# Turned value products with reciprocals through memory in the first attention, and the second attention's first score rounds among its last output products

## What is computed

```python
# first attention: H = 16 heads of D = 64, phi(x) = elu(x) + 1, written as a scan over positions
Q = _phi((x @ Wq + bq).reshape(bs, n, H, D)).transpose(1, 0, 2, 3)
K = _phi((x @ Wk + bk).reshape(bs, n, H, D)).transpose(1, 0, 2, 3)
V = (x @ Wv + bv).reshape(bs, n, H, D).transpose(1, 0, 2, 3)
...
    num = jnp.einsum('bhd,bhde->bhe', qi, KV)
    den = jnp.einsum('bhd,bhd->bh', qi, Ks)
    return ((KV, Ks), num / (den[..., None] + EPS))
...
return out @ Wo + bo
# second attention: 16 heads of 16, keys and values are the context itself
energy = jnp.einsum('nqhd,nkhd->nhqk', q, k)
energy = jnp.where(mask == 0, jnp.float32(-1e+20), energy)
attn = jax.nn.softmax(energy / jnp.sqrt(jnp.float32(EMB)), axis=-1)
out = jnp.einsum('nhqk,nkhd->nqhd', attn, v).reshape(N, Q, EMB)
return out @ W_out.T
```

## Time and profile before

| | |
|---|---|
| median of three runs | 1427.04 us |
| profiled execution | 1428.32 us |
| its span | 1426.3 us |
| TensorE busy | 1361.6 us (95%) |
| VectorE busy | 732.8 us (51%) |
| ScalarE busy | 515.3 us (36%) |
| GpSimd busy | 286.3 us (20%) |
| first attention, first to last projection pair | 13.5 to 331 us |
| second attention, batches in steady state | 14.6 us each |

### The profile page before, as it was taken

One profiled execution on the slowest core, in us unless ns is written; L12 is line 12 of the kernel. 1 busy time (PEld: TensorE's weight loads), 2 busy tenths in 40 slices (PEclk: granted clock), 3 DMA queues, 4 the chain that ended last, 5 costly groups with the idle time before them and its releaser, 6 DMA issues.

```text
span 1426.3 us, 30313 instructions
## 1 busy us (share of the span) xinstructions
PE 1361.6 (95%) x12024; PEld 955.1 (67%) x12024; DVE 732.8 (51%) x1762; ACT 515.3 (36%) x1004; POOL 286.3 (20%) x380
## 2 busy tenths in 40 slices
PE   6999999998999999889998999999999899999996
PEld 5888888885566666556664466575757677777764
DVE  5665555554566665367753122011112555678886
ACT  2212111221455555446654422122121444444444
POOL 2000000101111112388844000000000200124421
PEclk9999999998899999999999999999999999999999
DMA  6300000001222220012200100000000000000001
GB/s 205 62 13 0 1 1 1 1 1 35 46 48 63 53 59 24 2 43 74 62 17 10 56 0 0 0 1 0 0 0 0 3 3 4 13 17 16 16 6 53
DMA packets 35984, 36.04 MB, mean 25 GB/s; under 512 B 11696, under 2 KB 32544, under 8 KB 35856
## 3 DMA queue, kind: packets, MB, share of 16 engines
q1 hardware_dynamic: 35856, 34.23, 9.3%
HBM read 31.61 MB, written 1.86 MB: 23 GB/s over the span
## 4 chain that ended last, share of the span: by engine, by line
PE 67%; ACT 3%; DVE 2%; issue 2%; POOL 2%; DMA 0%; SPq 0%; DVEq 0%; ACTq 0%; POOLq 0%
PE banks L270 32%; PE banks L704 7%; PE banks L688 4%; PE banks L869 3%; PE banks L811 3%; PE banks L824 3%; PE banks L864 3%; PE banks L805 2%; PE banks L720 2%; PE banks L263 2%; ACT area L1248 2%; PE banks L852 2%; ACT area L1325 1%; POOL area L1109 1%; PE banks L762 1%
## 5 line engine op out<-in xcount | busy, mean ns | idle before, releaser
L1582 DVE TENSOR_REDUCE Y_room<-banks 112x2 f32<-112x750 f32 x128 | 115.5, 936 | 91.4 <-PE banks L688 91.4
L1658 DVE TENSOR_REDUCE area<-banks 112x8 f32<-112x896 f32 x96 | 100.2, 1086 | 76.6 <-PE banks L811 76.6
L1248 ACT ACTIVATE area<-banks,Y_room 125x896 f32<-125x896 f32 x96 | 96.7, 1007 | 95.3 <-PE banks L704 95.3
L1325 ACT ACTIVATE area<-banks 112x896 f32<-112x896 f32 x96 | 82.8, 914 | 121.1 <-PE banks L869 121.1
L270 PE MATMUL banks<-room,area 128*112 128x256 f32 (+1 forms) x384 | 118.3, 458 | 0.7 <-ACT area L1180 0.7
L1798 DVE SCALAR_TENSOR_TENSOR X<-banks,area,X 112x192 f32 (+1 forms) x64 | 26.5, 417 | 160.0 <-PE banks L270 160.0
L704 PE MATMUL banks<-room,area 64*125 64x224 f32 x768 | 102.6, 387 | 4.8 <-ACT area L1248 3.3
L1381 ACT ACTIVATE room<-banks 128x448 f32<-128x448 f32 x72 | 39.2, 544 | 183.3 <-PE banks L270 183.3
L270 PE MATMUL banks<-area,room 128*128 128x224 f32 x512 | 100.9, 359 | 2.0 <-ACT area L1200 2.0
L249 POOL TENSOR_TENSOR rstd<-mv,kcol 112x1 f32<-112x1 f32 x32 | 6.1, 192 | 469.1 <-DVE mv L1421 469.1
L270 PEld LDWEIGHTS banks<-area,room 128*128 128x128 f32 x512 | 98.1, 194 | 2.7 <-ACT area L1200 2.3
(11 more groups left out here) (233 smaller groups left out, 2497.0 us busy)
## 6 DMA issues: line engine op xcount, KB each, us to landing
Y_room<-in_ctx SPq DMA_DIRECT2D x16, 375.0 KB
area<-in_ctxT SPq DMA_DIRECT2D x64, 93.8 KB
l<-in_l SPq DMA_DIRECT2D x2, 1024.0 KB, 6.3
room<-in_ctxT SPq DMA_DIRECT2D x16, 112.0 KB, 2.2
out<-X SPq DMA_DIRECT2D x16, 112.0 KB, 1.9
X<-in_x SPq DMA_DIRECT2D x1, 1568.0 KB, 17.6
room<-in_Wq SPq DMA_DIRECT2D x1, 1024.0 KB, 5.0
room<-in_Wk SPq DMA_DIRECT2D x1, 1024.0 KB, 8.2
```

The lines of the kernel that those rows point to most:

```text
L1248: a_.activation(b_pT[g][:, c, :, :], banks[0:KC, 4:6, 0:QN], ACT.Exp, bias=b_bias[v][:, c:c + 1]).then_inc(Bs["ex"].sem, 1)
L1325: a_.activation(c_pT[:, i * 8 * S:(i + 1) * 8 * S].rearrange("p (j n) -> p j n", j=2), banks[0:S, 2 + 2 * i:4 + 2 * i, 0:4 * S], ACT.Exp). ...
L1582: v_.tensor_reduce(b_nb[u][:, 4 * a + k:4 * a + k + H + 1:H], banks[0:S, 2 * a:2 * a + 2, 0:SC], AX_X, ALU.max, negate=True).then_inc(Bs[" ...
L1658: v_.tensor_reduce(c_nb[:, 8 * i:8 * i + 8].rearrange("q (j n) -> q j n", j=2), banks[0:S, 2 + 2 * i:4 + 2 * i, 0:4 * S].rearrange("q j (n ...
```

## The change

In the first attention the value product is turned. `weighted_a(b)` now takes the values of a head as weights (112 x 64) and streams the masked scores, two heads side by side in column groups, so that the result comes out as `a_oT` wants it. The denominators come from sixteen products with `a_one`, a tile with one column of ones in each block of 32, four side by side, into bank 6. VectorE's `denominators` adds 1e-6 and takes the reciprocals, 128 x 112. SyncE's `reciprocals(b)` writes them to `den_scratch` in memory, waits, and loads them twice, each time repeated over 64 partitions, into `a_bc`. `normalised` multiplies banks 4 and 5 with `a_bc` straight into `a_oT`. `turned_a`, its copies on ScalarE and the nine bf16 products in it are gone.

The order is changed with it. The output product of an even batch comes after the next pair's query projections, followed by the odd batch's value products; the odd batch's output product comes after the keys, scores and values of the next pair's first batch. The transposes of the normed x go to bank 7 instead of bank 0.

At the seam, `queries_b(-1)` stands in the last pair, and `scores_b(0, ...)` and `queries_b(0)` stand between the output product of batch 14, the value products of batch 15 and what follows. The output product of batch 15 and its residual stand in `phase_b(1)`. GpSimd's filling of context areas 2 and 3 stays behind the residual of batch 15. In SyncE's list `reciprocals(0)` stands ahead of the mask's scratch, and `reciprocals(1)` to `reciprocals(15)` between `context(1)` and the wait for `ctx2`.

VectorE's program follows: behind `phase_a` it runs the residual of batch 14, the maxima of batch 0, the denominators of batch 15, `queries(0)` and at the end `normalised(15)`. The semaphores `t` and `h1` of a later block are now further counts of `A["sc"]` and `A["bc"]`.

```diff
@@ -388,6 +390,18 @@
             bcast(sp, bo0, "bo", ld["bo"])
             sp.dma_start(mask_i[:, :], T["mask"]).then_inc(ld["mask"].sem, 16)
             wload(sp, wx0[:, :, :], "W_out", ld["wx"])
+            def reciprocals(b):
+
+                sp.wait_ge(A["rd"].sem, A["rd"].at(b + 1))
+                sp.dma_start(den_scratch, a_rd).then_inc(A["sc"].sem, 16)
+                sp.wait_ge(A["sc"].sem, 16 * (b + 1))
+                sp.wait_ge(A["nm"].sem, A["nm"].at(2 * b))
+                rows = den_scratch.rearrange("(r c) s -> r c s", r=4)
+                for e in range(2):
+                    src = rows[:, 2 * e:2 * e + 2, :].rearrange("r c s -> r (c s)").partition_broadcast(LD)
+                    sp.dma_start(a_bc[LD * e:LD * e + LD, :].rearrange("p (r n) -> p r n", r=4), src).then_inc(A["bc"].sem, 16)
+
+            reciprocals(0)
             sp.wait_ge(pre["rowbias"].sem, 1)
             sp.dma_start(mask_scratch, mask_f[:, :]).then_inc(pre["scratch"].sem, 16)
             wload(sp, wqk1[:, :, 0:D], "wq", ld["c1"])
@@ -420,6 +434,8 @@
             sp.wait_ge(pre["bx"].sem, 1)
             for n in range(2):
                 context(n, n)
+            for b in range(1, B):
+                reciprocals(b)
             sp.wait_ge(pre["ctx2"].sem, 1)
             for n in range(2, 4):
                 context(n, n)
...
+            def weighted_a(b):
+
+                pe.wait_ge(A["sm"].sem, A["sm"].at(4 * b + 4))
+                pe.wait_ge(A["nm"].sem, A["nm"].at(2 * b))
+                pe.wait_ge(A["pj"].sem, A["pj"].at(12 * (b // 2) + 10 + 2 * (b % 2)))
+                if b == 0:
+                    pe.wait_ge(pre["av"].sem, 2)
+                for c in range(4):
+                    for r in range(4):
+                        h = 4 * r + 2 * (c % 2) + c // 2
+                        last = T3.matmul(pb[6][32 * r:32 * r + 32, 0:S], a_one[:, 32 * c:32 * c + 32], a_at[:, h * S:(h + 1) * S],
+                                         start=(c == 0), stop=(c == 3), tile_position=(0, 32 * r))
+                last.then_inc(A["ds"].sem, 1)
+                for m in range(8):
+                    for e in range(2):
+                        h = 2 * m + e
+                        last = T3.matmul(pb[4 + m // 4][LD * e:LD * e + LD, (m % 4) * S:(m % 4 + 1) * S], a_v[:, h, :],
+                                         a_at[:, h * S:(h + 1) * S], start=True, stop=True, tile_position=(0, LD * e))
+                last.then_inc(A["nd"].sem, 1)
...
-                    for h in range(H):
-                        n = h // 6
-                        o = (h - NUM[n][0]) * (LD + 1)
-                        last = T3.matmul(pb[4 + n][0:S, o:o + LD + 1], a_at[:, h * S:(h + 1) * S], a_v[:, h, :],
-                                         start=True, stop=True)
-                        if h + 1 == NUM[n][1]:
-                            last.then_inc(A["nd"].sem, 1)
-
...
-                    pe.wait_ge(A["xte"].sem, A["xte"].at(p + 1))
-                    for g in range(8):
-                        project(wk0 if g > 3 else wq0, g, 2 * (g % 4))
-                    scores(0, 0)
-                    values(0)
+                pe.wait_ge(A["xte"].sem, A["xte"].at(p + 1))
+                for g in range(4):
+                    project(wq0, g, 2 * g)
                 if p > 0:
-                    turned_a(2 * p - 1)
-                if p < B // 2:
-                    scores(0, 1)
-                if p > 0:
-                    output(2 * p - 1)
+                    output_a(2 * p - 2)
+                    weighted_a(2 * p - 1)
+                for g in range(4):
+                    project(wk0, 4 + g, 2 * g)
+                scores(0, 0)
+                values(0)
                 if p == 2:
-                    pe.wait_ge(A["xu"].sem, A["xu"].at(2 * p))
+                    pe.wait_ge(A["xu"].sem, A["xu"].at(2 * p - 1))
                     pe.wait_ge(pre["rowbias"].sem, 1)
                     for c in range(NKC):
                         last = T3.transpose(pb[7][0:KC, c * B:(c + 1) * B], mask_f[:, c * KC:(c + 1) * KC], ident[0:B, 0:B])
                     last.then_inc(Bs["kt"].sem, 1)
-                if p < B // 2:
-                    weighted_a(0)
-                    scores(1, 0)
-                    values(1)
-                    turned_a(2 * p)
-                    scores(1, 1)
-                    if p == 2:
-                        pe.wait_ge(Bs["ke"].sem, 1)
-                    output(2 * p)
-                    if p + 1 < B // 2:
-                        normed(p + 1)
-                    weighted_a(1)
-
-            pe.wait_ge(ld["id"].sem, 16)
-            for p in range(B // 2 + 1):
-                phase_a(p)
+                scores(0, 1)
+                if p == 2:
+                    pe.wait_ge(Bs["ke"].sem, 1)
+                if p > 0:
+                    output_a(2 * p - 1)
+                weighted_a(2 * p)
+                scores(1, 0)
+                values(1)
+                if p + 1 < B // 2:
+                    normed(p + 1)
...
+                if b == 1:
+                    pe.wait_ge(Bs["me"].sem, Bs["me"].at(1))
+                    output_a(B - 1)
...
+                    pe.wait_ge(pre["b6"].sem, 1)
+                    keep_busy(6, 3)
+                if b == 1 and k < 2:
+                    keep_busy(6, 3)
 
...
-            pe.wait_ge(A["xu"].sem, A["xu"].at(B))
-            keep_busy(5, 4)
+            pe.wait_ge(ld["id"].sem, 16)
+            for p in range(B // 2):
+                phase_a(p)
+            pe.wait_ge(Bs["qs"].sem, Bs["qs"].at(1))
+            output_a(B - 2)
+            pe.wait_ge(pre["masks"].sem, 1)
+            scores_b(0, 0, 0, 0)
+            weighted_a(B - 1)
+            scores_b(0, 1, 0, 0)
+            queries_b(0)
+            scores_b(0, 2, 0, 0)
+            scores_b(0, 3, 0, 0)
...
-                if isinstance(b, int) and b == -1:
+                if isinstance(b, int) and b == 0:
                     pool.wait_ge(A["xu"].sem, A["xu"].at(B))
                     g_.memset(area[:, B_OWN:B_OWN + 2 * QUAD * SCP], 1.0).then_inc(pre["ctx2"].sem, 1)
...
                 ln_apply(A, b, a_xn[b % 2], 2, (A["xt"], b // 2)).then_inc(A["xn"].sem, 1)
+
+            def denominators(b):
+
+                dve.wait_ge(A["ds"].sem, A["ds"].at(b + 1))
+                v_.tensor_scalar(a_den, pb[6][:, 0:S], 1e-6, None, ALU.add).then_inc(A["den"].sem, 1)
+                dve.wait_ge(A["den"].sem, A["den"].at(b + 1))
+                v_.reciprocal(a_rd, a_den).then_inc(A["rd"].sem, 1)
+
+            def normalised(b):
+
+                dve.wait_ge(A["bc"].sem, 32 * (b + 1))
+                dve.wait_ge(A["nd"].sem, A["nd"].at(b + 1))
+                dve.wait_ge(A["wd"].sem, A["wd"].at(b))
+                for n in range(2):
+                    c = slice(n * 4 * S, (n + 1) * 4 * S)
+                    v_.tensor_tensor(a_oT[:, c], pb[4 + n][:, 0:4 * S], a_bc[:, c], ALU.mult).then_inc(A["nm"].sem, 1)
...
                 for g in range(8):
+                    if p > 0 and g == 2:
+                        normalised(2 * p - 2)
+                    if p > 0 and g == 4:
+                        phi_of(3)
+                        residual_a(2 * p - 2)
+                        denominators(2 * p - 1)
                     z_of(g)
-                    if g:
...
                     dve.wait_ge(ld["cst"].sem, 16)
                 masked(0, 0)
                 masked(0, 1)
...
+                    normalised(2 * p - 1)
                 v_of(0, 0)
                 v_of(0, 1)
                 masked(0, 2)
                 masked(0, 3)
+                if more:
+                    normed(2 * p + 2)
                 if p > 0:
                     residual_a(2 * p - 1)
-                if more:
-                    normed(2 * p + 2)
-                normalised(2 * p)
+                denominators(2 * p)
                 if more:
                     stats_of(A, 2 * p + 3, 1, 0)
+                else:
+                    stats_of(Bs, 0, 1, 0)
                 masked(1, 0)
                 masked(1, 1)
-                v_of(1, 0)
-                v_of(1, 1)
-                masked(1, 2)
-                masked(1, 3)
                 if more:
                     normed(2 * p + 3)
                 else:
-                    stats_of(Bs, 0, 1, 0)
-                residual_a(2 * p)
+                    phase_b(-1, 1, -1)
+                v_of(1, 0)
+                v_of(1, 1)
+                if not more:
+                    normalised(2 * p)
+                masked(1, 2)
+                masked(1, 3)
                 if p == 0:
```

186 lines of the change are left out of this document (87 added, 99 removed).

## The result

The changed kernel took 1428.88 us in the median of 20 executions (1427.14 to 1433.05), the kernel before 1426.7 in as many (1424.49 to 1428.95): a ratio of 1.0017, with a 95% interval of 1.0011 to 1.0024. The forecast was 1421.2, within 1411 to 1432. The time is inside the range, but it moved the other way than forecast: 2.2 us longer instead of 5.8 shorter.

The account below looks back on a forecast made before the run. TensorE's instructions were taken to set the first attention's time. Pairs of 36.52 us and 12.8 us lost at batch 1 put the last pair at 276.2; the 69.1 us seam gave -5.8, so 1421.2 us, range 1411 to 1432.

Parts of the forecast that it names:

- turned value product: First attention, TensorE: value products two side by side in column groups, 60 ns each, 32 per batch, 1.92 us.
- gap at batch 1: First attention: TensorE stalls 10.3 us near 68 us, as batch 1's scratch write queues behind mask, weight and context transfers.
- gap and colder clock together: Batch 1: the 10.3 us stall plus 2.5 us lost at half clock behind it, 12.8 us, once.
- low bound: Turned value products: a transpose streaming 112 columns alone takes 108 ns, so two side by side take no less than 54 each.
- value of the neighbours: Turned value products: four-wide rows and the scores, both with tiles side by side, come to 60 ns.
- round trip: First attention: 5.7 us for write and broadcasts, covered by about 12 us of TensorE work; rival, over 11.5 us: slower, 0.06.
- sum of 69.1 us: Seam: last pair's start to the first turned product, against 66.2 us before, some 9 us with TensorE idle.
- 4 us worse: Rival at the seam: the clock falls before the last output product; -2 us in all, no measurable change; chance 0.15.
- Residual, memset, ten context loads: Seam, behind output 15: residual 0.4 us, GpSimd's filling 2.60 us, SyncE's ten context loads 4.8 us.
- a price of 69 ns with a bad seam: Upper end of the range: two-wide products at 69 ns together with a bad seam, given as +5 us, 1432.
- The write of batch 1: Rival: batch 1's scratch write passes the waiting transfers, lands at 66, stall 3 us; -13 us in all; chance 0.12.
- the weight loads stayed hidden: Rivals, two-wide products: loads not hidden, old spacing of 97 to 102 ns, +15 us, 0.09; load plus stream, +47, 0.02.

Follow-up runs that it names:

- e2: Changed kernel with all of batch 1's reciprocals issued ahead of the values and contexts of batches 0 and 1: 1415.19 us, 13.7 less than the changed kernel.
- e3: Changed kernel with batch 1's reciprocals behind the contexts of batches 0 and 1 but ahead of their values: 1420.27 us, 8.6 less than the changed kernel.
- e1: Changed kernel with batch 0's four maxima transfers issued ahead of the memset wait and contexts 2 and 3: 1415.20 us, 13.7 less than the changed kernel.
- e9: The changed kernel run and profiled once more, not edited: 1428.83 us, ratio 1.001 to the kernel before.
- e10: Changed kernel with maxima and batch 1's reciprocals moved ahead, batch 0's values spread before the memset, and more seam fillers: 1393.90 us, ratio 0.9768 to the kernel before.
- e7: Changed kernel with only the weave undone: batch 15's value and output products again ahead of the second attention's first scores, memset back in place: 1426.43 us.
- e5: Changed kernel without the four groups of three filler products between the second attention's first score rounds: 1426.96 us, ratio 1.0005 to the kernel before.
- e8: Kernel before with one edit, batch 0's four maxima transfers issued ahead of the memset wait and contexts 2 and 3: 1427.36 us, ratio 1.0002.

## Why the prediction was wrong

**The first attention was right.** Each step against its value:

| step | forecast | measured |
|---|---|---|
| ones, per instruction | 30 ns | 28 ns |
| turned value product | 60 ns | 53 ns |
| a pair | 36.52 | 36.28 |
| end of the first pair | 43.8 | 43.55 |
| gap at batch 1 | 10.3 | 12.13 |
| gap and colder clock together (12.13, and 5.25 for 3.7) | 12.8 | 13.7 |
| last pair's start | 276.2 | 275.37 |

The 53 ns lie at the low bound, 54, which was half a transpose, and not at the value of the neighbours. The weight loads of the same products, in groups by shape from 20 to 330 us, mean ns of one behind the comma:

```profile
L533 PEld LDWEIGHTS banks<-area 112*64 112x64 f32 x512 | 24.6, 137 | 2.7 <-issue 2.7
L527 PEld LDWEIGHTS banks<-area 112*32 112x32 f32 x512 | 11.7, 110 | 6.8 <-issue 5.4 <-DVE area L1481 1.4
```

With one row group the products are spaced 53 and 28 ns apart, where a single weight load takes 137 and 110 ns. The rule of the Trainium skill (page TensorE: Matmul & The Clock Gate, section The mechanism) that weight loads overlap with matmuls in flight only when their row group differs is not borne out by this; the same section also names a background weight buffer as a target of loads that run ahead, and no run here tells which way these loads took. Of the round trip, no pair but the second shows a gap, as forecast; write and broadcasts are issued 1.56 us apart in the steady part (196.51 and 198.07). For batch 1 the mechanism was the one named, a small write behind the values' and contexts' bytes, and e2 and e3 show it; its gap was 1.8 us longer than forecast, since the write landed at 74.1 and not at 73.2, and the broadcasts took until 78.6.

**The seam was mis-sized, and this is the step that failed.** Its mechanism was named (contexts ahead of the maxima) and e1 confirms it, but the sum of 69.1 us came out as 75.6. From the rows of the changed kernel, the terms were:

- Last pair's start to the end of output 14: 40.6 forecast, 316.26 - 275.37 = 40.9 measured.
- From there to output 15, the maxima and the normalising: 13.6 forecast, 333.25 - 316.26 = 17.0 measured, +3.4 (18.1 in e9). Two things are in it. First, `normalised(15)` ends at 329.69 + 1.15 = 330.84, 1.0 us late. I had carried over the 11.4 us of before, which were measured with a filled TensorE; in the changed order it stands 2.42 us for the queries, the granted clock goes from 1.00 (320 to 325 us) to 0.53 (325 to 330), and the rounds of 0.90 us take 2.4. Second, the last output product does not follow at once, but 2.4 us later: in TensorE's program it stands behind the first score round of batch 1, three fillers and the turning of the maxima with ScalarE's copy (L647, L1237). The sum had put this at nothing. In e10, at full clock, the whole stretch takes 317.65 - 302.01 = 15.6 us, of which the second part is still 1.8.
- Output 15 and the transpose: 3.8 forecast, 338.02 - 333.25 = 4.8 measured, +0.9 (6.0 in e9), again the clock (3.71 us in e10). I had given a term to the clock at the first gap but none here, although the rival "4 us worse" named it.
- Residual, memset, ten context loads: 341.24 and 346.18 are within 0.4 us of the forecast lengths.
- The maxima's transfers: 3.3 forecast, 351.01 - 346.18 = 4.8 measured, +1.5. The 3.3 us were read where nothing was in flight ahead of them (DMA share 0.00 from 345 to 348 us in the kernel before); here the ten context loads were, with a share of 1.16 from 345 to 346. That these are the cause is argued from the shares and was not run by itself; in e1 nothing waits for the transfers.

Together, with 0.3 and 0.4 us from the first and fourth, +6.5 us. Against the forecast the last pair starts 0.8 us earlier, so the first turned product lies at 351.0 and not at 345.3, and all of the forecast 5.8 us is gone. Of the rivals the worse seam came true, at 6.5 us where I had given it 4, and only in part by the clock that it named; so it took the whole gain. That the measured time still lies in the range is not the forecast's merit: the range was wide, and its upper end, a price of 69 ns with a bad seam, adds up to +2.8 us by its own terms and not to +5. The write of batch 1 did not pass the waiting transfers, the weight loads stayed hidden, and no later pair waited for the round trip.

**The last 2.2 us are explained only in part.** At the first turned product the changed kernel is level with the kernel before (351.01, 351.14), and at GpSimd's mark, at 1100.8 us, still within 0.4. Then comes the second fall of the clock, at 1115, and it has a price. From the mark to TensorE's last product the changed kernel takes 1418.23 - 1100.83 = 317.4 us and e9 317.5; the kernel before takes 1416.73 - 1100.46 = 316.3, e7 316.3, e5 and e8 316.2, all with a granted clock of 1.00 from 1115 to 1120. So the second fall goes with 1.1 to 1.2 us, where no instruction was changed. It does not follow the seam's length: e9, with the first turned product at 352.4, has it, e5 and e7, at 352.4 and 352.2, do not. What brings it is open. The spans of the two profiled executions are only 0.4 us apart because that of the kernel before ends 9.6 us behind its last product, the changed one 8.5. The profiled execution of the kernel before also lies 1.6 us over its median, and its executions spread over 1423.95 to 1431.25 us. So about half of the 2.2 us is found, and the rest stays open.

## What to carry to other kernels

When work is moved, follow every semaphore wait of an issuing queue past which it is moved: an in-order queue turns a wait that was long over (the memset, in the kernel before) into one on which urgent small transfers depend, and moving them ahead in e1 gave 13.7 us, where the change as it was made had gained nothing. A small round trip through memory belongs ahead of the bulk loads in the program: here it landed only behind their bytes, even when the engines were two thirds idle (10.2 us, and 2.8 ahead of them). When a product is put into another place of an engine's program, everything that stands before it there belongs into the sum, also where its data are ready. And a stage's measured pace holds with the clock at which it was measured: where the change opens idle stretches on TensorE, the stages behind them are to be priced at both clocks, or the stretches filled.

## What the runs showed of the hardware

- With column groups side by side in f32, the weight loads (137 and 110 ns a record) do not set the spacing: two wide 53 ns, four wide 28 ns for 112 streamed columns, against 102 ns for the old product with 112 weight columns and 65 streamed.
- A 56 KB write took 10.2 us to land behind two 375 KB loads of 125 rows and the contexts, 3.9 behind the contexts only, 2.8 ahead of both, and 1.5 in the median.
- After a gap of 5 us the next 3.7 us product took 5.2 (e3), after one of 12 us 5.25: between these two the price of the lower clock hardly grew with the gap.
- Without the groups of three fillers behind the score rounds the seam took 76.3 us (e5), with them 75.6 and 77.5; with eight in the idle stretch and seven behind the rounds the granted clock stayed at 2.4 GHz through it (e10).
- The same kernel, profiled twice, had its last output product at 4.85 and at 6.02 us, and its seam at 75.6 and 77.5: where in a stage the clock falls and returns differs from one execution to the next.
